# A dense count loop without scatters beside it, in rounds of five, on one core of Trainium2

## Chip, cores and metric

One core of a Trainium2 chip runs the whole program. The metric is the device time of one launch in microseconds (us). The engines are named as in the profile: PE is TensorE (PEld its weight loads), DVE is VectorE, ACT is ScalarE, POOL is GpSimd, SP is the engine that issues most DMA transfers. A q behind a name (DVEq) is that engine's sequencer, which reads instructions, waits on semaphores and loads registers.

## The reference

Four blocks of a graph network with dense layers between them, on x of 3125 nodes by 256 columns and one list of 50,000 edges (src, dst):

```python
x = x + _L0_gnn_ref(_layernorm(x), ..., edge_index)           # two GCN layers over (src, dst)
x = x + _L0_ffn_ref(_layernorm(x)[None], ..., L0_ffn_edge_index)[0]   # a GAT over 32,768 own edges gates 4 experts
x = x + _L1_gnn_ref(_layernorm(x), ..., node_type_4, edge_type_8, src, dst)   # HGT attention
x = x + _L1_ffn_ref(_layernorm(x)[None], ...)[0]              # soft mixture of 8 experts with two hidden layers
x = x + _L2_gnn_ref(_layernorm(x), ..., edge_index)           # SAGE over dst -> src
x = x + _L2_ffn_ref(_layernorm(x)[None], ...)[0]
x = x + _L3_gnn_ref(_layernorm(x), edge_weight, ..., src, dst)  # weighted sum over edges, by src
x = x + _L3_ffn_ref(_layernorm(x)[None], ...)[0]
```

Three orders of edges are needed: the common edges by dst (first GCN and HGT), the 32,768 own edges of the GAT by their dst, and the common edges by src (the weighted sum near the end).

## The kernel before

**Sorting.** An `EdgeSort` computes for every edge the place it has in the sorted list. The list `edge` is then put in order inside the chip. The lists `own` and `back` are put in order by scatters: an indirect DMA issued by POOL writes one column of 128 records (16 bytes each) to their places in DRAM. `own` has 256 such columns and `back` has 391, so 647 scatters in all. The method `send(pool, lo, hi, pace)` issues the columns lo to hi, and behind each one POOL clears a small "pace" buffer of 128x320 numbers, which spaces the scatters in time. The records and addresses that the scatters read must stay in SBUF until they are sent: those of `own` lie in the first of the four large buffers (`bufs[0]`), those of `back` in `back_space`, 128x1955 numbers. The sorted lists come back with `fetch()`: `own` right behind the GCN, `back` late, behind the SAGE block.

**Where the scatters stand.** They are handed out as `beside` functions, which POOL runs in a block of the program while the other engines do that block's work. A block ends for all engines when the last one is through, POOL too. Before the change: `own` 0 to 158 beside the sorts and the first GCN steps; `own` 158 to 256 and `back` 0 to 100 beside the counts; `back` 100 to 160 and 160 to 205 beside the two GCN passes; `back` 205 to 391 beside the experts of the GAT block, and there POOL goes on with `order.write`, the list of nodes by type for HGT.

**The counts.** `build_counts` makes the dense 3200x3200 matrix that says how many edges run from each source to each target. The sorted edges are in groups of 128. A "visit" is one group in one half of the sources for one tile of targets: there are 440 visits. For each visit DVE makes two one-hot matrices from the edges' ends, a narrow one (`hot_d`, L742, 128x128) and a wide one (`hot_s`, L749, 128x1600), and PE multiplies them in four matmuls (L767: 512, 512, 512 and 64 columns), adding into PSUM. When a tile and half (a "bucket", 50 of them, so 8.8 visits each) is done, ACT copies it out (L783), clears the PSUM region (L786) and narrows the copy to 16 bits (L787); SP stores both. There are two PSUM regions, one for each half.

**Rounds.** The loop runs in rounds of RING visits, two rounds to one turn of the loop. At the start of each round DVE's sequencer loads the visits' numbers (bucket and column) into registers from SBUF (the helper's line L96), PE's sequencer loads its own (region), and DVE makes the round's `hot_d`. `hot_s` has RING buffers: a `hot_s` waits until PE is done with the visit RING places earlier, and until ACT has cleared the region that its bucket wants. These waits stand on DVE's sequencer, so everything behind them on DVE waits too, the next round's register loads among them.

Of the kernel before, what the change touches and what calls it, by code (L numbers as in the profile page):

```python
# [6 lines left out]
F32 = mybir.dt.float32  # L7
# [4 lines left out]
I32 = mybir.dt.int32  # L12
# [5 lines left out]
P = 128  # L18
N = 3125
D = 256  # L20
NT = -(-N // P)
# [12 lines left out]
PACE = 320  # L34
# [25 lines left out]
def gather_sems(nc, stage, what, n):  # L60

    return [nc.alloc_semaphore(f"{stage}_{what}{u}") for u in range(n)]
# [111 lines left out]
def alloc_edges(nc, ctx, name, n_edges, like=None, split=False):  # L174


    most = (n_edges + NT * (P - 1)) // P
    groups = -(-most // (R * DEEP)) * R * DEEP
    e = EdgeList()
    e.name, e.groups, e.split = name, groups, split  # L180
    if like is None:
        e.rec = ctx.enter_context(nc.sbuf_tensor(f"{name}_rec", [P, groups, 4], F32))
        e.src = ctx.enter_context(nc.sbuf_tensor(f"{name}_src", [P, groups], I32))
        e.key = ctx.enter_context(nc.sbuf_tensor(f"{name}_key", [P, groups], I32))
    else:
        e.rec, e.src, e.key = (t[:, 0:groups] for t in (like.rec, like.src, like.key))
    e.tile = ctx.enter_context(nc.sbuf_tensor(f"{name}_tile", [P, groups], F32))
    e.blk = ctx.enter_context(nc.sbuf_tensor(f"{name}_blk", [1, groups], I32))
    e.end = ctx.enter_context(nc.sbuf_tensor(f"{name}_ends", [1, NT], I32))
    e.filled = ctx.enter_context(nc.sbuf_tensor(f"{name}_filled", [P, NT], F32))  # L190
    if split:
        e.visits = -(-(most + NT) // 8) * 8
        e.visit_bucket = ctx.enter_context(nc.sbuf_tensor(f"{name}_visit_bucket", [1, e.visits], I32))
        e.visit_group = ctx.enter_context(nc.sbuf_tensor(f"{name}_visit_group", [1, e.visits], I32))
        e.visit_end = ctx.enter_context(nc.sbuf_tensor(f"{name}_visit_end", [1, 2 * NT], I32))
    e.dram = nc.dram_tensor(f"{name}_sorted", (P * groups + GROUPS_MAX, 4), F32).ap()
    return e


class EdgeSort:  # L200
# [15 lines left out]
    def __init__(self, nc, kit, name, e, dst, space, bufs, inside=False):  # L216
        self.nc, self.kit, self.name, self.e, self.bufs = nc, kit, name, e, bufs
        self.rested, = gather_sems(nc, name, "rested", 1)
        self.rests = 0
        self.dst, self.n = dst, dst.shape[0]  # L220
        self.C = C = -(-self.n // P)
        self.inside = inside
        if inside:
            self.to_part, self.to_group, self.low, self.high = (space[:, k * C:(k + 1) * C] for k in range(4))
            self.rec = self.adr = None
        else:
            self.rec = space[:, 0:C * 4].rearrange("p (c w) -> p c w", w=4)
            self.adr = space[:, C * 4:C * 5].bitcast(I32)
            self.sent = gather_sems(nc, name, "sent", self.SENDS)
# [318 lines left out]
    def send(self, pool, lo, hi, pace=None):  # L548
# [13 lines left out]
        if hi == self.C:  # L562
            for u in range(self.SENDS):
                pool.wait_ge(self.sent[u], 16 * -(-(self.C - u) // self.SENDS))

    def put_inside(self, space, beside):

        nc, kit, e, C, groups = self.nc, self.kit, self.e, self.C, self.e.groups
        BATCH, RING = 8, 8
# [110 lines left out]
def build_counts(nc, kit, e, counts, counts16, bufs, beside):  # L680
# [6 lines left out]

    groups, visits = e.groups, e.visits
    COLUMNS = groups + 1
    RING, OUT = 4, 3  # L690
    BASE = RING + 1
    REGION = 2048
    WIDE = NP - FIRST_HALF
# [1224 lines left out]
    return ap2d.rearrange("e (k p) -> p (e k)", p=P)  # L1918


def soft_moe_stage(nc, kit, A, x, bufs, rdeg_dram):


    b2 = bufs[1]
# [3 lines left out]
    with ExitStack() as c:  # L1928
# [3 lines left out]
        gates = sb("gates", [P, NT, E])  # L1932
# [8 lines left out]
        with ExitStack() as cc:  # L1941
# [5 lines left out]
            with nc.Block() as block:  # L1947
# [31 lines left out]
                def _(act):  # L1979
                    for k, n in enumerate("12"):  # L1980
# [5 lines left out]
        of = lambda name: lambda e: A[name][ds(e, 1), :, :]  # L1986
        expert_mlps(nc, "soft", b2, E, [Mid(of("L1_ffn_W1"), 2, fc, ACT.Relu, par["b1"], par["v1"]),
                                        Mid(of("L1_ffn_W2"), fc, fc, ACT.Relu, par["b2"], par["v2"])],
                    of("L1_ffn_Wo"), bo, gates, x, stats=kit.stats)


BIG = 1e30
# [1954 lines left out]
def program(nc, A, out):  # L3947

    with ExitStack() as ctx:
        kit = Kit()  # L3950
# [16 lines left out]
        with ExitStack() as pair:  # L3967
            bufs = [pair.enter_context(nc.sbuf_tensor(n, [P, NT * D], F32)) for n in ("big1", "big2")] + [big3, big4]
            with ExitStack() as c:
# [1 line left out]
                own = alloc_edges(nc, c, "own", own_dst.shape[0])  # L3971
                n_all = -(-A["src"].shape[0] // P) * 5
                back_space = c.enter_context(nc.sbuf_tensor("back_space", [P, n_all], F32))
                pace = {n: c.enter_context(nc.sbuf_tensor(f"{n}_pace", [P, PACE], F32))[:] for n in ("own", "back")}
                paced = lambda lo, hi, which: lambda pool: which.send(pool, lo, hi, pace)
                with ExitStack() as cc:

# [12 lines left out]
                    back_sort.prepare(A["dst"], weight=A["edge_weight"], beside=paced(105, 145, own_sort))  # L3990
                    g = gcn_first(nc, kit, A, cc, x, bufs, paced(145, 152, own_sort), paced(152, 158, own_sort))

                    def rest(pool):
                        own_sort.send(pool, 158, own_sort.C, pace)
                        back_sort.send(pool, 0, 100, pace)
                    build_counts(nc, kit, edges, counts, counts16, bufs, rest)
                    scale_and_heavy_nodes(nc, kit, g)
                    gcn_stage(nc, kit, g, x, bufs, counts, counts16, counts_t, paced(100, 160, back_sort),
                              paced(160, 205, back_sort))
                    own_sort.fetch()  # L4000
                order.find(A["node_type_4"], c)

                def send_and_order(pool):
                    back_sort.send(pool, 205, back_sort.C, pace)
                    order.write(pool)
                gat_moe_stage(nc, kit, A, x, bufs, own, send_and_order)
            hgt_stage(nc, kit, A, x, bufs, edges, order)
            soft_moe_stage(nc, kit, A, x, bufs, rdeg_dram)
        sage_stage(nc, kit, A, x, big3, big4, counts16, rdeg_dram)
        back_sort.fetch()  # L4010
        with ExitStack() as pair:
# [96 lines left out]
```

## Time and profile before

| | us |
|---|---|
| median of 3 runs | 6159.12 (6157.68 to 6162.46) |
| the profiled execution, its own time | 6162.04 |
| its span in the trace | 6160.4 |
| counts, from the first to the last visit | 537 to 939 of the span |
| experts of the GAT block | 1869 to 2229 |
| experts of the soft mixture | 3611 to 4153 |

The profile is of one execution. The page gives the busy time of each engine over the span and in 40 slices of 154 us; the trace can be asked for a stretch (busy time by engine), for groups of instructions by line, for what each engine waited for, and for single instructions in order of time. In a row "[1.43 <-issue]" is idle time of that engine just before, and what ended it; "issue" is a wait for nothing that the profile shows.

### The profile page before, as it was taken

The page shows a single profiled execution, that of the slowest core. Times are in us where ns is not written, and L with a number is a line of the kernel's source. Part 1 is how long each engine was busy: PE and PEld are TensorE (multiplying, and loading weights), DVE is VectorE, ACT ScalarE, POOL GpSimd, SP SyncE. Part 2 cuts the span into 40 slices and gives each one's busy share as a digit, 9 for nine tenths or more (in the row PEclk, how much of TensorE's full clock was granted, in tenths as well). Part 3 has the DMA queues.
Part 4 walks back from the last instruction along what each step waited for, and adds up shares of the span by engine and source line. Part 5 has one row for each costly group of instructions (what it writes and reads, how often), then busy time and mean ns, then how long its engine had stood idle before and what let it go on. Part 6 is the DMA issues. An engine that isn't in the chain of part 4 may idle for free. (4 is left out here: it accounts for less than half of the span.)

```text
span 6160.4 us, 89090 instructions
## 1 busy us (share of the span) xinstructions
PE 4547.2 (74%) x22985; PEld 3258.0 (53%) x23041; DVE 3500.1 (57%) x7298; ACT 1667.5 (27%) x3845; POOL 2410.6 (39%) x2714
## 2 busy tenths in 40 slices
PE   5866777945558979566659889999999395455558
PEld 1213444634446755345536677778888353355546
DVE  8988993556683245699948634441112333655544
ACT  0863553511102225111100233333222121200022
POOL 0747876527707833577600000001111301477700
PEclk8998998955558989788859989999999597677779
DMA  0002346712210038999947210004333321233400
GB/s 31 2 11 75 153 158 205 230 25 34 32 63 22 8 88 332 316 330 322 286 135 237 79 23 10 10 15 143 99 106 103 96 102 53 70 102 104 99 18 21
DMA packets 392065, 669.88 MB, mean 109 GB/s; under 512 B 115851, under 2 KB 280850, under 8 KB 387242
## 3 DMA queue, kind: packets, MB, share of 16 engines
q1 hardware_dynamic: 295938, 420.30, 21.6%
q0 software_dynamic: 95744, 247.14, 13.0%
q8 instruction: 88, 1.44, 0.1%
q14 instruction: 103, 0.84, 0.0%
q10 hardware_dynamic: 192, 0.15, 0.0%
HBM read 438.59 MB, written 228.81 MB: 108 GB/s over the span
## 5 line engine op out<-in xcount | busy, mean ns | idle before, releaser
L3370 POOL CAST sagel_piece<-x 128x1792 fp32r<-128x1792 f16 (+1 forms) x75 | 112.8, 1503 | 1557.1 <-DMA x<-counts 1137.1
L555 POOL DMA_INDIRECT back_sorted<-back_space x391 | 411.4, 1052 | 240.9 <-POOLq L1758 170.8
L1072 POOL DMA_INDIRECT wsum_a_rows<-table,edge_src x416 | 411.8, 990 | 220.0 <-issue 118.5
L1086 PE MATMUL wsum_a_ps<-wsum_a_hot,wsum_a_rows 128*128 128x128 f32 x1664 | 310.7, 363 | 246.3 <-DMA wsum_a_rows<-table,edge_src 139.7
L2172 POOL DMA_INDIRECT big<-hgt_table,edge_key x416 | 393.3, 945 | 176.4 <-issue 131.1
L1086 PEld LDWEIGHTS wsum_a_ps<-wsum_a_hot,wsum_a_rows 128*128 128x128 f32 x1664 | 285.7, 267 | 271.2 <-DVE big L1113 218.0
L3426 PE MATMUL sagel_ps<-sagel_piece,sagel_high 128*128 128x448 f32 x1050 | 397.8, 379 | 0.8 <-issue 0.8
L555 POOL DMA_INDIRECT own_sorted<-big x256 | 273.3, 1068 | 311.2 <-issue 310.2
L767 PE MATMUL cnt_ps<-cnt_hot_s,cnt_hot_d 128*128 128x512 bf16 (+1 forms) x1705 | 305.9, 333 | 107.3 <-DVE cnt_hot_s L749 107.1
L3426 PE MATMUL sagel_ps<-sagel_piece,sagel_low 128*128 128x448 f32 x1050 | 383.9, 366 | 0.0
L2220 PE MATMUL hgt_s_pq<-big 128*128 x1248 | 230.6, 350 | 167.8 <-DVE hgt_s_tmp L2259 134.0
L2172 POOL DMA_INDIRECT big<-gat_table,own_src x288 | 272.3, 946 | 90.5 <-issue 86.2
L749 DVE TENSOR_SCALAR cnt_hot_s<-cnt_iota,cnt_source 128x1600 bf16<-128x1600 int16 x440 | 303.3, 748 | 1.6 <-ACT cnt_ps L786 0.9
L767 PEld LDWEIGHTS cnt_ps<-cnt_hot_s,cnt_hot_d 128*128 128x128 bf16 x1760 | 161.0, 97 | 252.1 <-issue 130.3
L1882 ACT ACTIVATE soft_h<-soft_ps,soft_b,soft_v 128x320 f32<-128x320 f32 x320 | 197.5, 617 | 334.6 <-PE soft_ps L1848 334.6
L2220 PEld LDWEIGHTS hgt_s_pq<-big 128*128 128x128 bf16 x1248 | 145.6, 117 | 236.5 <-issue 187.5
L2249 DVE TENSOR_REDUCE hgt_highest<-hgt_s_pm 128x1024 f32 (+1 forms) x208 | 252.6, 1215 | 0.1
L624 ACT ACTIVATE big<-big 128x128 f16<-128x128 f16 x782 | 228.4, 384 | 22.0 <-DVE big L595 22.0
L2610 PE MATMUL hgt_a_ps<-hgt_a_val,hgt_a_hot 128*128 128x260 f32 x832 | 211.8, 398 | 27.6 <-DVE hgt_a_val L2589 25.6
L1903 DVE TENSOR_TENSOR soft_answer<-soft_py,soft_bo 128x256 f32<-128x256 f32 x200 | 82.8, 414 | 247.1 <-PE soft_py L1860 247.1
L3426 PEld LDWEIGHTS sagel_ps<-sagel_piece,sagel_high 128*128 128x128 f32 x1050 | 197.6, 188 | 18.8 <-issue 1.8
L3426 PEld LDWEIGHTS sagel_ps<-sagel_piece,sagel_low 128*128 128x128 f32 x1050 | 197.7, 188 | 16.6
(977 smaller groups left out, 10773.7 us busy)
## 6 DMA issues: line engine op xcount, KB each, us to landing
hgt_edge_values<-big SPq DMA_DIRECT2D x104, 512.0 KB
big<-hgt_edge_values SPq DMA_DIRECT2D x104, 512.0 KB, 4.5
x<-counts SPq DMA_DIRECT2D x75, 448.0 KB, 3.3
x<-counts SPq DMA_DIRECT2D x75, 336.0 KB, 2.9
counts<-big SPq DMA_DIRECT2D x25, 832.0 KB
counts<-big SPq DMA_DIRECT2D x25, 768.0 KB
big<-counts SPq DMA_DIRECT2D x30, 640.0 KB
counts_turned<-big SPq DMA_DIRECT2D x30, 640.0 KB, 4.0
```

The source lines that it names most:

```text
L555: self.nc.gpsimd.indirect_dma_start(self.e.dram, bass.IndirectOffsetOnAxis(ap=self.adr[:, c:c + 1], axis=0), self.rec[:, c, :], None).then ...
L624: nc.scalar.activation(valued[k % RING][:, n, :], parts[b % 2][:, k % BATCH, :], ACT.Copy, scale=value[:, k:k + 1]).then_inc(weighed, 1)
L749: nc.vector.tensor_scalar(hot_s[u][:], iota16[:], source[:, ds(places[u], 1)], None, ALU.is_equal).then_inc(matched, 1)
L767: mm = nc.tensor.matmul(ps[:, ds(regions[u] + lo, n)], hot_d[h][:, u, :], hot_s[u][:, lo:lo + n], start=False, stop=False, skip_group_chec ...
L1072: nc.gpsimd.indirect_dma_start(rows[n % DEEP][:, u, :], None, table, bass.IndirectOffsetOnAxis(ap=e.src[:, g:g + 1], axis=0)).then_inc(gat ...
L1086: mm = nc.tensor.matmul(ps[r.slot % 2][u][:, k * P:(k + 1) * P], rows[r.slot][:, u, k * P:(k + 1) * P], hot[r.slot % 2][:, u, :], start=Tr ...
L1882: nc.scalar.activation(h[n][:, f, half * CHUNK:(half + 1) * CHUNK], ps[g % RING][:, 0:CHUNK], m.func, bias=bias, scale=scale).then_inc(rea ...
L2172: nc.gpsimd.indirect_dma_start(rows[n % DEEP][:, u, :], None, at.table, bass.IndirectOffsetOnAxis(ap=at.index[:, g:g + 1], axis=0)).then_i ...
L2220: mm = nc.tensor.matmul(pq_v[:, u, :], hot_t[nxt.slot][:, u, :], part[:, ds(blocks[u], 1), :].rearrange("p o w -> p (o w)"), start=(k == 0 ...
L2249: nc.vector.tensor_reduce(highest[:, :, ds(old.n * R + 2 * pair, 2)], pm[pair][:].rearrange("p (g h n) -> p h g n", g=2, h=H), AX_X, ALU.m ...
L2610: nc.tensor.matmul(ps[:, ds(regions[u], W)], hot[k % 2][:, u, :], val[k % 2][:, u, :], start=False, stop=False, skip_group_check=True).the ...
L3426: mm = nc.tensor.matmul(ps[BANKS[half][n]][:, 0:w], part[:, t, f * P:(f + 1) * P], piece, start=(t == 0 and m == 0), stop=(t == NT - 1 and ...
```

## The change

Five edits:

1. No scatter stands beside the counts any more. In their place POOL writes the records of `back` from `back_space` to DRAM (`keep`) and moves those of `own` from the large buffer into `back_space` (`take_up`), which is so one buffer for both lists.
2. The counts have RING = 5: five `hot_s` buffers, rounds of five visits. The number of visits is rounded up to a multiple of 10 in place of 8, and is 440 either way; the loop has 44 turns in place of 55.
3. `own` 158 to 214 and 214 to 256 go beside the two GCN passes (56 and 42 scatters in place of 60 and 45).
4. The GAT block's experts first get the records of `back` again from DRAM, and have `back` 0 to 186 beside them (186 scatters, as before).
5. The soft mixture's experts, which had nothing beside them, read the records into a new buffer `back_space_too` and have `back` 186 to 391 beside them (205 scatters).

```diff
@@ alloc_edges
-        e.visits = -(-(most + NT) // 8) * 8
+        e.visits = -(-(most + NT) // 10) * 10
@@ EdgeSort
+    def keep(self, pool, space):
+        self.kept_by = self.nc.dram_tensor(f"{self.name}_kept", (P, 5 * self.C), F32).ap()
+        self.move(pool, space, self.kept_by)
+
+    def take_up(self, pool, space, kept_by=None):
+        C = self.C
+        self.rec = space[:, 0:C * 4].rearrange("p (c w) -> p c w", w=4)
+        self.adr = space[:, C * 4:C * 5].bitcast(I32)
+        self.move(pool, self.kept_by if kept_by is None else kept_by, space)
+
+    def move(self, pool, from_, to):
+        self.moves += 1
+        pool.dma_start(to, from_).then_inc(self.moved, 16)
+        pool.wait_ge(self.moved, 16 * self.moves)
@@ build_counts
-    RING, OUT = 4, 3
+    RING, OUT = 5, 3
@@ soft_moe_stage
-                    of("L1_ffn_Wo"), bo, gates, x, stats=kit.stats)
+                    of("L1_ffn_Wo"), bo, gates, x, beside=beside, stats=kit.stats)
@@ program
-                pace = {n: c.enter_context(nc.sbuf_tensor(f"{n}_pace", [P, PACE], F32))[:] for n in ("own", "back")}
+                pace_one = c.enter_context(nc.sbuf_tensor("pace", [P, PACE], F32))
+                pace = {n: pace_one[:] for n in ("own", "back")}
-                    def rest(pool):
-                        own_sort.send(pool, 158, own_sort.C, pace)
-                        back_sort.send(pool, 0, 100, pace)
-                    build_counts(nc, kit, edges, counts, counts16, bufs, rest)
+                    def put_away(pool):
+                        back_sort.keep(pool, back_space[:])
+                        own_sort.take_up(pool, back_space[:, 0:n_own], bufs[0][:, 0:n_own])
+                    build_counts(nc, kit, edges, counts, counts16, bufs, put_away)
                     scale_and_heavy_nodes(nc, kit, g)
-                    gcn_stage(nc, kit, g, x, bufs, counts, counts16, counts_t, paced(100, 160, back_sort),
-                              paced(160, 205, back_sort))
+                    gcn_stage(nc, kit, g, x, bufs, counts, counts16, counts_t, paced(158, 214, own_sort),
+                              paced(214, own_sort.C, own_sort))
                     own_sort.fetch()
                 def send_and_order(pool):
-                    back_sort.send(pool, 205, back_sort.C, pace)
+                    back_sort.take_up(pool, back_space[:])
+                    back_sort.send(pool, 0, 186, pace)
                     order.write(pool)
-            soft_moe_stage(nc, kit, A, x, bufs, rdeg_dram)
+            with ExitStack() as c:
+                back_space = c.enter_context(nc.sbuf_tensor("back_space_too", [P, n_all], F32))
+                pace_too = {"back": c.enter_context(nc.sbuf_tensor("back_pace_too", [P, PACE], F32))[:]}
+                def send_rest(pool):
+                    back_sort.take_up(pool, back_space[:])
+                    back_sort.send(pool, 186, back_sort.C, pace_too)
+                soft_moe_stage(nc, kit, A, x, bufs, rdeg_dram, send_rest)
```

The order of DVE's instructions at the start of a round of the counts, before; L96 is the register load, L740 a wait, and each ISA row is the part of the next instruction that puts a register into its address:

```order
L96 TENSOR_LOAD cnt_column0
L740 REGISTER_ALU
L742 ISA
L742 TENSOR_SCALAR cnt_hot_d1<-cnt_iota0,cnt_target0 128x128
L742 ISA
L742 TENSOR_SCALAR cnt_hot_d1<-cnt_iota0,cnt_target0 128x128
L742 ISA
L742 TENSOR_SCALAR cnt_hot_d1<-cnt_iota0,cnt_target0 128x128
L742 ISA
L742 TENSOR_SCALAR cnt_hot_d1<-cnt_iota0,cnt_target0 128x128
```

The same place in the changed kernel, whose lines stand 20 lower:

```order
L96 TENSOR_LOAD cnt_column0
L760 REGISTER_ALU
L762 ISA
L762 TENSOR_SCALAR cnt_hot_d1<-cnt_iota0,cnt_target0 128x128
L762 ISA
L762 TENSOR_SCALAR cnt_hot_d1<-cnt_iota0,cnt_target0 128x128
L762 ISA
L762 TENSOR_SCALAR cnt_hot_d1<-cnt_iota0,cnt_target0 128x128
L762 ISA
L762 TENSOR_SCALAR cnt_hot_d1<-cnt_iota0,cnt_target0 128x128
L762 ISA
L762 TENSOR_SCALAR cnt_hot_d1<-cnt_iota0,cnt_target0 128x128
```

The loads stand there once for five visits, and the first wide one-hot of the round comes behind five narrow ones in place of four.

POOL's instructions around the counts in the changed kernel (the IOTA belongs to the counts' first block, L3300 is the first step behind them; `big` is the large buffer that held `own`):

```order
L734 IOTA big 128x1600
L731 UNCONDITIONAL_BRANCH
L821 UNCONDITIONAL_BRANCH
L583 DMA back_kept<-back_space 128x1955
L583 DMA back_space<-big 128x1280
L735 UNCONDITIONAL_BRANCH
L54 ISA x15
L1612 UNCONDITIONAL_BRANCH
L3300 DMA big<-counts,heavy_at 24x3200
```

Before, 198 pairs of a scatter (L555) and a clear (L560) stood between those branches where the two transfers stand now. And POOL's instructions at the start of the soft mixture's experts, where before it had none; L2192 is the last gather of HGT:

```order
L2192 DMA big<-hgt_table,edge_key 128x512 x416
L2160 UNCONDITIONAL_BRANCH
L54 ISA x72
L1836 UNCONDITIONAL_BRANCH
L583 DMA back_space_too<-back_kept 128x1955
L556 DMA back_sorted<-back_space_too 53688x4
L561 MEMSET back_pace_too 128x320
L556 DMA back_sorted<-back_space_too 53688x4
L561 MEMSET back_pace_too 128x320
```

The transfer stands ahead of the scatters, and they wait for it.

## Rows read from the trace of the kernel before

**Rows 1.** The page: the span.

```profile
span 6160.4 us, 89090 instructions
```

**Rows 2.** Busy time by engine: the counts, their part with scatters, their part without.

```profile
core 0: us, PE busy (x) PEld busy (x) DVE busy (x) ACT busy (x) POOL busy (x), PEclk, DMA share, GB/s
537.00:939.00 402.00, 305.94 (x1705) 161.04 (x1760) 389.34 (x880) 223.88 (x199) 320.79 (x388) 0.99 0.39 152
545.00:890.00 345.00, 262.91 (x1474) 139.72 (x1521) 344.12 (x762) 194.83 (x173) 310.51 (x376) 1.00 0.40 154
894.00:934.00 40.00, 31.99 (x180) 16.15 (x185) 34.12 (x95) 22.30 (x20) 0.00 (x0) 1.00 0.40 163
```

**Rows 3.** DVE's one-hots, 545 to 890 us: busy us, mean ns, idle before.

```profile
L749 DVE TENSOR_SCALAR cnt_hot_s<-cnt_iota,cnt_source 128x1600 bf16<-128x1600 int16 x380 | 267.9, 763 | 0.0
L742 DVE TENSOR_SCALAR cnt_hot_d<-cnt_iota,cnt_target 128x128 bf16<-128x128 int16 x382 | 93.1, 514 | 1.4 <-PE cnt_ps L767 1.0 <-issue 0.3
```

**Rows 4.** Both one-hots, 894 to 934 us.

```profile
L749 DVE TENSOR_SCALAR cnt_hot_s<-cnt_iota,cnt_source 128x1600 bf16<-128x1600 int16 x48 | 27.3, 631 | 0.9 <-ACT cnt_ps L786 0.9
L742 DVE TENSOR_SCALAR cnt_hot_d<-cnt_iota,cnt_target 128x128 bf16<-128x128 int16 x47 | 8.7, 250 | 4.9 <-PE cnt_ps L767 4.9
```

**Rows 5.** PE's weight loads in order of time, beside scatters: one round, x16.

```profile
862.52 2.58 PEld L767 LDWEIGHTS cnt_ps<-cnt_hot_s,cnt_hot_d 128*128 128x128 bf16 x16 [1.07 <-issue]
```

**Rows 6.** The same behind the last scatter: half a round, then five rounds.

```profile
899.98 1.24 PEld L767 LDWEIGHTS cnt_ps<-cnt_hot_s,cnt_hot_d 128*128 128x128 bf16 x8
902.65 2.58 PEld L767 LDWEIGHTS cnt_ps<-cnt_hot_s,cnt_hot_d 128*128 128x128 bf16 x16 [1.43 <-issue]
905.55 2.58 PEld L767 LDWEIGHTS cnt_ps<-cnt_hot_s,cnt_hot_d 128*128 128x128 bf16 x16 [0.32 <-issue]
909.19 2.58 PEld L767 LDWEIGHTS cnt_ps<-cnt_hot_s,cnt_hot_d 128*128 128x128 bf16 x16 [1.06 <-issue]
912.29 2.58 PEld L767 LDWEIGHTS cnt_ps<-cnt_hot_s,cnt_hot_d 128*128 128x128 bf16 x16 [0.52 <-issue]
916.25 2.58 PEld L767 LDWEIGHTS cnt_ps<-cnt_hot_s,cnt_hot_d 128*128 128x128 bf16 x16 [1.38 <-issue]
```

**Rows 7.** Register loads of four numbers and of one, 894 to 934 us: ns min/median/max.

```profile
L96 PEldq TENSOR_LOAD <-cnt_region x12: 329/332/930, 894.6 to 932.2; - x12
...
L96 ACTq TENSOR_LOAD <-edge_visit_end x5: 274/278/382, 898.2 to 925.4; - x5
```

**Rows 8.** GAT experts in order of time: POOL's first scatter, first step behind the scatters, last step.

```profile
1869.27 1.00 POOL L555 DMA_INDIRECT back_sorted<-back_space  x1 [170.84 <-POOLq L1758]
...
2160.52 1.63 POOL L2989 DMA_DIRECT2D type_list<-type_none  x1 [1.76 <-issue]
...
2224.86 0.29 POOL L2997 TENSOR_SCALAR type_source<-type_at 128x28 int32<-128x28 int32 x1 [3.93 <-DMA type_at<-type_list]
```

**Rows 9.** PE there: first matmul, a group beside scatters, one behind them.

```profile
1875.90 11.16 PE L1848 MATMUL gatx_ps<-big,gatx_w 128*128 x32 [28.72 <-DMA gatx_wl<-in_L_ffn_W_dram]
...
1912.78 8.78 PE L1848 MATMUL gatx_ps<-big,gatx_w 128*128 x32
...
2192.04 8.78 PE L1848 MATMUL gatx_ps<-big,gatx_w 128*128 x32
```

**Rows 10.** DVE's last work in that block.

```profile
2228.36 0.43 DVE L1911 BATCH_NORM_STATS2 row_stats<-x  x1
```

**Rows 11.** A transfer from DRAM: KB, us from issue to landing.

```profile
edge_rec<-back_sorted SPq DMA_DIRECT2D x1, 832.0 KB, 4.3
```

**Rows 12.** Soft mixture: PE's first matmul, and its first matmul behind the block.

```profile
3616.22 7.09 PE L1848 MATMUL soft_ps<-big,soft_w 128*128 x16 [12.02 <-DMA soft_wl<-in_L_ffn_Wo_dram]
...
4153.52 0.47 PE L874 MATMUL sage_ln_ps<-ident,sage_ln_st 128*128 128x128 f32 x1 [9.14 <-DVE sage_ln_st L846]
```

**Rows 13.** Second GCN pass: POOL's last clear, DVE's last work.

```profile
1231.41 0.38 POOL L560 MEMSET back_pace<- 128x320 f32 x1
...
1241.41 0.89 DVE L1734 TENSOR_TENSOR big<-gcn_ps,big 128x512 f32<-128x512 f32 x2 [0.59 <-PE gcn_ps L1368]
```

More of the change, by code:

```diff
@@ L218, in __init__ @@
         self.rested, = gather_sems(nc, name, "rested", 1)
-        self.rests = 0
+        self.rests = self.moves = 0
+        self.moved, = gather_sems(nc, name, "moved", 1)
         self.dst, self.n = dst, dst.shape[0]
@@ L1918, in columns, with soft_moe_stage @@
     return ap2d.rearrange("e (k p) -> p (e k)", p=P)
-def soft_moe_stage(nc, kit, A, x, bufs, rdeg_dram):
+def soft_moe_stage(nc, kit, A, x, bufs, rdeg_dram, beside):
     b2 = bufs[1]
```

## The prediction, as recorded before the run

> **What bounds the kernel now.** The page first: the span of 6160.4 us [rows 1] is a row of stages, one behind the other, so what an edit is worth is read in the stage that it touches. The stage at stake is the counts, from 537 to 939 us. I read it by stretches: 402 us for 440 visits, with DVE busy for 389.34 of them and PE for 305.94 [rows 2]. POOL's scatters end some 45 us ahead of the counts (POOL is busy for 310.51 of 345 us, then for 0.00 of 40 [rows 2]), so this trace holds both cases: beside scatters (545 to 890) and without (894 to 934).
>
> Beside scatters DVE is busy for 344.12 of 345 us and makes 380 wide one-hots, 0.908 us for each visit [rows 2, 3]. It is the bound: a round in PE's row of weight loads is 2.58 us of work and 1.07 us of waiting, 3.65 us for four visits [rows 5]. Without scatters the same instructions are shorter. A wide one-hot takes 631 ns in place of 763, a narrow one 250 in place of 514 [rows 3, 4]. Rows overlap a little, so I go by DVE's busy time: 34.12 us for 48 visits [rows 2, 4], which is 0.711 us a visit. If that alone decided, 440 visits would take 313 us. But DVE then stood idle for 5.9 of the 40 us, 4.9 of it behind PE [rows 4]: the bound has moved into the hand-over between the two.
>
> PE's rows without scatters show how. Eight loads (two visits) take 1.24 us and sixteen 2.58, so a visit is 0.67 us of PE [rows 6]. Between rounds PE stands still for a short time in the middle of a turn (0.32 and 0.52 us) and a long one at the loop's branch (1.43, 1.06, 1.38, mean 1.29). Four rounds, 902.65 to 916.25, take 13.60 us: 0.85 us a visit. That is nearer to PE's 0.67 than to anything that DVE needs, and the loss is at the edges of rounds.
>
> **What the change does to the counts.** Two parts.
>
> *No scatters.* This alone would give the pace of the clean stretch: 0.85 times 440 is 374 us, a gain of 28. The 48 visits in 40 us (0.833) would give 367.
>
> *Rounds of five.* The loads and the branch come once in five visits, and DVE may be five visits ahead of PE in place of four. Why the second counts: DVE's last wide one-hot of a round waits until PE is done with the round before, on DVE's sequencer; only then can the sequencer go on to the branch, the two register loads, and the next round's narrow one-hots. With four places PE has four visits (2.7 us) of work left at that moment. What DVE has to do till the next round can start is two loads (0.34 us each at the median of such a load, 0.94 at worst, as PE's and DVE's are alike), the narrow one-hots (8.7 us over 47, 0.18 each, so 0.7), one wide one (0.63) and the branch: 2.4 to 3.4 us, so it is late at some branches. With five places PE has 3.35 us left against 2.6 to 3.6. It should be late rarely, and then PE's own gap decides. In the middle of a turn that is 0.42 (mean of 0.32 and 0.52); at the branch it lies between 0.42 and 1.29, and I take the middle, 0.85, since part of the 1.29 is DVE's lateness. A round of five is 2.58 + 0.67 = 3.25 us of loads, so a turn is 2 x 3.25 + 0.42 + 0.85 = 7.77 us for ten visits, 0.777 a visit, 342 us in all. With the gap of 1.29 kept it is 0.821 and 361 us. Slow register loads still happen (930 ns at worst against 329 at best [rows 7]), so I put the counts at 348 us: 54 less than 402.
>
> A register load takes 333 ns for four numbers (332 in this stretch) and 278 for one [rows 7], so a fifth costs about 18 ns, nothing against a saved load in five. The Trainium skill, Runtime: NRT & Kernel Launch, Instruction fetch mechanics, puts a register load at about 200 ns for each register. By that a round of five would save nothing on the loads, since five numbers cost 1.0 us where four cost 0.8, and DVE would be late at every branch: that is the first rival below. The rows here show under half of that price at four numbers, and nearly none for the fifth.
>
> *The two transfers.* `keep` and `take_up` in the counts are 1.0 MB and 0.66 MB. The nearest row is 832 KB landed in 4.3 us [rows 11]; with queueing I allow 15 us for both. They lie beside 348 us of counts in which POOL has nothing else, so they cost 0; without that cover it would be those 15. ACT, which must clear a region before DVE goes on, was busy for 22.3 of 40 us [rows 2] and held DVE back for 0.9 [rows 4].
>
> **The other stages.**
>
> *GCN.* 56 and 42 scatters for 60 and 45. In the second pass POOL's last clear is at 1231.41 and DVE's last work of the pass at 1241.41 [rows 13]. Fewer scatters end no later, even with the wait for the last landings, so 0.
>
> *GAT experts.* The records (1.0 MB) must come back ahead of the first scatter. Scaled from 832 KB in 4.3 us it would be 5.2, and it is issued beside 2 MB of expert weights, so I take 9 us. POOL starts its scatters that much later than 1869.27. It is nearly the last in this block: its last step is at 2224.86 to 2225.15, DVE's at 2228.36 to 2228.79 [rows 8, 10]. It gets 1.8 us back, the wait for landed scatters ahead of `type_list` [rows 8], which now comes elsewhere. So POOL ends at 2225.15 + 9 - 1.8 = 2232.4, 3.5 us behind DVE's old end. DVE's own end moves too: PE waits for its first weights until 1875.90 [rows 9], and a third of the traffic more delays it by 2 to 3 us. The two delays lie side by side, so the larger counts: +3.5 us (0 if the transfer takes 5 us, +8 if 13). HGT, which waits for this block, starts that much later.
>
> *Soft mixture.* 205 scatters more. In the GAT's experts 186 took 289.5 us (from 1869.27 to 2160.52 less its wait of 1.76 [rows 8]), 1.56 each, so 319 us and the transfer; the block lasts from 3616.22 to about 4153 [rows 12], 537 us. POOL is through 200 us early. What do scatters do to the others there? In the GAT block a group of 32 matmuls takes 8.78 us beside scatters and 8.78 behind them [rows 9]. PE binds, and is not slowed. So only the transfer beside the first weights costs, +2.5 us (0 to 4).
>
> **The sum.** -54 + 0 + 3.5 + 2.5 = -48 us. Against the profiled execution: span 6160.4 to 6112.4, own time 6162.04 (1.6 outside the span) to 6114. That execution stands 2.9 above the median of 6159.12, so the forecast for the median is 6111 us.
>
> **The rivals.**
>
> *The fifth place brings nothing (17 in 100).* The counts take the clean stretch's pace, 367 to 374 us, a little less for 22 branches in 110 saved. For it: DVE's loads at a branch take up to 0.94 us each, and PE's gap there may be all its own. Against it: the mid-turn gaps are 0.3 to 0.5, with the same loads and no branch. Gain 28 to 35, less 6: 6130 to 6137 us.
>
> *DVE's pace alone (8 in 100).* All gaps vanish behind the fifth buffer and the counts take 313 us. For it: DVE's 0.711 is the longer of the two bare times. Against: PE's sequencer can't start a round's matmuls ahead of its own load. 6159 - 89 + 6 = 6076 us.
>
> *ACT becomes the bound (4 in 100): no change.* DVE, five visits ahead, runs into the wait for the cleared region at each of the 50 buckets. At the 0.9 us of [rows 4] each, 45 us of the 54 are lost: 6156. Against: a bucket has 8.8 visits, about 6.9 us, while ACT's busy 22.30 us for 48 visits [rows 2] are 4.1 us a bucket.
>
> *Slower (4 in 100): the soft experts suffer.* If scatters held DVE or ACT there as they hold DVE in the counts, PE would wait for free PSUM banks in each of 40 groups of five tiles. It decides from 1.2 us a group (48 / 40) and at 2 us a group the time is 6111 + 80 = 6191. For it: wide one-hots are 21% longer beside scatters [rows 3, 4]. Against: 8.78 and 8.78 [rows 9].
>
> **How the numbers follow.** The forecast case has 67 in 100 and gives 6095 to 6126 (counts 332 to 361, the two transfers 1 to 9). What a measurement of this kernel can tell from no change is about 0.2%, 12 us. The first rival reaches to 6140, and with part of the second the range is 6086 to 6140; out of it lie most of the second, the third and the fourth. Faster by over 0.2%: 67 + 17 + 8, less a little, 91 in 100. Within 0.2%: 5. Slower: 4.
>
> **What would show it.** Counts from first to last visit near 348 us; wide one-hots at 631 ns throughout; PE's gaps 0.3 to 0.5 in mid-turn and below 1 at the branch; POOL's last step behind DVE's in the GAT block; the groups of matmuls in the soft experts as long with scatters as they were without. The prediction is wrong if branch gaps stay at 1.3, if DVE waits for ACT in most buckets, or if a stage that the change doesn't touch runs at another clock.

## The result and the profile after

The changed kernel takes 6243.21 us (median of 4 runs, 6237.74 to 6249.4) where the kernel before takes 6158.40 beside it: a ratio of 1.0137, 95% interval 1.0122 to 1.0152. It is 85 us slower; 6111 was forecast.

The page's span answers to [rows 1]:

```profile
span 6247.7 us, 88910 instructions
```

The busy time by stretch answers to [rows 2]; the last row is the whole of the counts, from the first narrow one-hot to the last weight load.

```profile
core 0: us, PE busy (x) PEld busy (x) DVE busy (x) ACT busy (x) POOL busy (x), PEclk, DMA share, GB/s
545.00:890.00 345.00, 245.16 (x1265) 115.73 (x1296) 236.43 (x648) 165.08 (x147) 0.00 (x0) 0.93 0.32 129
894.00:934.00 40.00, 27.18 (x136) 12.57 (x140) 27.21 (x77) 18.05 (x16) 0.00 (x0) 0.91 0.30 123
542.00:1016.00 474.00, 335.59 (x1714) 158.16 (x1759) 322.06 (x880) 220.86 (x196) 0.00 (x0) 0.92 0.31 127
```

POOL is idle, as planned, yet everybody else is idle more too: DVE for 109 of the 345 us in which it was busy throughout in [rows 2]. By the same measure (first narrow one-hot to last weight load) the counts took 398.4 us before and take 474.2 now, 76 more. The rest of the span's 87 us is small: 5 us lie ahead of the counts and come and go between executions (the counts begin at 536 or 541 us in runs with the same program up to there), 3 in the GAT experts, 3 in the soft mixture, some single ones elsewhere.

DVE's one-hots in the counts, by form, answer to [rows 3, 4]:

```profile
L769 DVE TENSOR_SCALAR cnt_hot_s<-cnt_iota,cnt_source 128x1600 bf16<-128x1600 int16 x436 | 246.1, 630 | 2.1 <-ACT cnt_ps L806 1.5 <-PE cnt_ps L787 0.3 <-issue 0.2
L762 DVE TENSOR_SCALAR cnt_hot_d<-cnt_iota,cnt_target 128x128 bf16<-128x128 int16 x435 | 78.6, 249 | 148.8 <-PE cnt_ps L787 104.2 <-issue 44.5
```

The work itself is what the forecast said: 630 and 249 ns. The 148.8 us of idleness ahead of the narrow one-hots is new, and PE waits for DVE in its turn. A chain that goes round between two engines, each idle, has something in it that is on neither engine's busy row. It is on the sequencers'. The register loads (ns min/median/max) answer to [rows 7]:

```profile
L96 DVEq TENSOR_LOAD <-edge_visit_bucket x87: 587/1187/2523, 543.9 to 1008.6; - x87
...
L96 DVEq TENSOR_LOAD <-cnt_column x87: 586/1189/2590, 545.2 to 1009.9; - x87
L96 PEldq TENSOR_LOAD <-cnt_region x87: 584/1236/2647, 546.4 to 1010.9; - x87
L96 ACTq TENSOR_LOAD <-edge_visit_end x49: 273/278/402, 552.9 to 999.7; - x49
```

A load of five numbers takes 584 ns at least and 1187 to 1236 at the median, where four took 333 to 346. It is not dear everywhere: sorted by where it begins, 17 of the 22 column loads that begin at a multiple of 16 bytes (every fourth round, since five numbers are 20 bytes) take under 1 us, and none of the other 66 takes less than 1181 ns. And the trace of before held it already, in a stage that the prediction never looked at: DVE's five loads of five numbers each in the GAT layer. In order of time they take 612, 1196, 1178, 1181 and 591 ns: the first and the last, which begin at byte 0 and byte 80 of their row, are the short ones.

```profile
L96 DVEq TENSOR_LOAD <-gat_t_last x5: 591/1178/1196, 1716.0 to 1722.6; - x5
```

PE's weight loads in order of time answer to [rows 6]:

```profile
675.80 3.25 PEld L787 LDWEIGHTS cnt_ps<-cnt_hot_s,cnt_hot_d 128*128 128x128 bf16 x20 [1.54 <-issue]
681.67 3.25 PEld L787 LDWEIGHTS cnt_ps<-cnt_hot_s,cnt_hot_d 128*128 128x128 bf16 x20 [2.62 <-issue]
687.86 0.49 PEld L787 LDWEIGHTS cnt_ps<-cnt_hot_s,cnt_hot_d 128*128 128x128 bf16 x3 [2.94 <-issue]
688.63 0.15 PEld L787 LDWEIGHTS cnt_ps<-cnt_hot_s,cnt_hot_d 128*128 128x128 bf16 x1 [0.28 <-issue]
689.05 0.21 PEld L787 LDWEIGHTS cnt_ps<-cnt_hot_s,cnt_hot_d 128*128 128x128 bf16 x2 [0.27 <-issue]
```

A round of five is 3.25 us of loads, to the hundredth what was forecast; the gaps are 1.5 to 2.9 us and not 0.4 to 0.9. Behind two such gaps the loads are suddenly 0.43 us apart. The granted clock beside them says why: 0.50 of full speed, 1.2 GHz, for these three microseconds, and 1.00 ahead of them and behind.

```profile
681.00:687.00 6.00, 3.33 (x19) 1.69 (x20) 3.49 (x10) 2.81 (x2) 0.00 (x0) 1.00 0.49 197
688.00:691.00 3.00, 3.00 (x10) 1.25 (x10) 2.64 (x9) 0.00 (x0) 0.00 (x0) 0.50 0.00 0
```

In the whole loop 151 loads follow the one before in their round by 0.3 to 0.45 us (8 in the kernel before), 102 of them within a visit and 49 from one visit to the next; together they are 30 us longer than at the usual distance. The lower clock follows PE's idleness here, and adds to the time.

### The profile page after: what moved, and what is told of

It reads as the page before. It is cut to its first block and busy times, and to the rows that moved or that the text cites. A ratio compares the mean times of both kernels' runs of the same rounds, so it can differ in the third digit from the quotient of the medians.

```text
span 6247.7 us, 88910 instructions
## 1 busy us (share of the span) xinstructions
PE 4597.9 (74%) x22996; PEld 3272.4 (52%) x23041; DVE 3442.6 (55%) x7298; ACT 1669.2 (27%) x3845; POOL 2370.5 (38%) x2718
## 5 line engine op out<-in xcount | busy, mean ns | idle before, releaser
L1106 PE MATMUL wsum_a_ps<-wsum_a_hot,wsum_a_rows 128*128 128x128 f32 x1664 | 328.1, 377 | 231.4 <-DMA wsum_a_rows<-table,edge_src 137.9
L2192 POOL DMA_INDIRECT big<-hgt_table,edge_key x416 | 393.8, 947 | 177.3 <-issue 131.7
L787 PE MATMUL cnt_ps<-cnt_hot_s,cnt_hot_d 128*128 128x512 bf16 (+1 forms) x1716 | 336.0, 356 | 153.0 <-DVE cnt_hot_s L769 152.4
L1106 PEld LDWEIGHTS wsum_a_ps<-wsum_a_hot,wsum_a_rows 128*128 128x128 f32 x1664 | 302.6, 281 | 256.9 <-DVE big L1133 184.7
L2192 POOL DMA_INDIRECT big<-gat_table,own_src x288 | 272.7, 947 | 90.5 <-issue 86.2
L556 POOL DMA_INDIRECT own_sorted<-big x158 | 164.9, 1044 | 293.7 <-issue 293.7
L769 DVE TENSOR_SCALAR cnt_hot_s<-cnt_iota,cnt_source 128x1600 bf16<-128x1600 int16 x440 | 248.3, 630 | 2.1 <-ACT cnt_ps L806 1.5
L556 POOL DMA_INDIRECT back_sorted<-back_space_too x205 | 208.6, 1018 | 40.9 <-issue 33.8
```

What stands on the lines that cost most here:

```text
L556: self.nc.gpsimd.indirect_dma_start(self.e.dram, bass.IndirectOffsetOnAxis(ap=self.adr[:, c:c + 1], axis=0), self.rec[:, c, :], None).then ...
L769: nc.vector.tensor_scalar(hot_s[u][:], iota16[:], source[:, ds(places[u], 1)], None, ALU.is_equal).then_inc(matched, 1)
L787: mm = nc.tensor.matmul(ps[:, ds(regions[u] + lo, n)], hot_d[h][:, u, :], hot_s[u][:, lo:lo + n], start=False, stop=False, skip_group_chec ...
L1106: mm = nc.tensor.matmul(ps[r.slot % 2][u][:, k * P:(k + 1) * P], rows[r.slot][:, u, k * P:(k + 1) * P], hot[r.slot % 2][:, u, :], start=Tr ...
L2192: nc.gpsimd.indirect_dma_start(rows[n % DEEP][:, u, :], None, at.table, bass.IndirectOffsetOnAxis(ap=at.index[:, g:g + 1], axis=0)).then_i ...
```

## The experiments

Theory A: the slower load of five numbers is the whole loss, because most rounds no longer begin at a multiple of 16 bytes (A1), or because of the fifth number itself (A2). Rivals: the counts without scatters have a slow pace of their own (B), or the fifth place is worth nothing (D). All runs in one table; the counts from the first narrow one-hot to the last weight load, the load being DVE's of `column` (or its copy) at the median, the clock from 545 to 890 us. Load, clock and counts are of one traced execution of each kernel; the ratio is of whole times.

| kernel | places, numbers a load, rounds a turn | scatters beside | load, ns | clock | counts, us | ratio to before, 95% |
|---|---|---|---|---|---|---|
| before | 4, 4, 2 | yes | 343 | 1.00 | 398.4 | 1 |
| changed | 5, 5, 2 | no | 1189 | 0.93 | 474.2 | 1.0137 (1.0122 to 1.0152) |
| e1_four | 4, 4, 2 | no | 343 | 1.00 | 372.0 | 0.9957 (0.9940 to 0.9973) |
| e2_five_beside | 5, 5, 2 | yes | 1187 | 0.94 | 480.5 | 1.0123 (1.0106 to 1.0140) |
| e3_rows_of_eight | 5, 5 aligned, 2 | no | 590 | 1.00 | 385.4 | 1.0008 (0.9994 to 1.0023) |
| e4_four_shifted | 4, 4 shifted, 2 | no | 966 | 0.91 | 529.0 | 1.0211 (1.0194 to 1.0228) |
| e5_fours_five_places | 5, 4, 10 | no | 342 | 1.00 | 345.5 | 0.9929 (0.9916 to 0.9942) |
| e7_fours_five_beside | 5, 4, 10 | yes | 345 | 1.00 | 394.5 | 1.0005 (0.9996 to 1.0013) |
| e8_fours_early_load | 5, 4, 10, PE's early | no | 343 | 1.00 | 348.5 | 0.9932 (0.9920 to 0.9945) |
| e10_fours_eight_places | 8, 4, 10 | no | 342 | 0.99 | 344.2 | 0.9931 (0.9914 to 0.9947) |
| e11_fours_ten_rounds | 4, 4, 10 | no | 342 | 1.00 | 354.9 | 0.9947 (0.9931 to 0.9964) |

The kernel before took 6520 us beside e1 to e4, 6593 beside e5, e7 and e8, and 6163 beside e10 and e11. At the first two of these levels stages with gathers from DRAM are longer (from HGT's first step to the first weight load of the soft mixture: 1387 us in the trace of before, 1555 in e2's, 1611 in e5's, 1390 in e11's), but not the counts. The cause isn't known: the chip is not enough for it, since e5 and e11 have the same chip on record. So the counts are compared in us, and whole times by their ratios.

### Undoing the five, undoing the removal: e1_four and e2_five_beside

```diff
-    RING, OUT = 5, 3
+    RING, OUT = 4, 3
```

> The changed kernel with rounds of four and four places for wide one-hots; everything else as changed. Theory A (a load of five numbers is what costs: 587 ns at least, 1182 to 1237 in most rounds, where four took 333 to 343): the loads are back at 333 to 343 ns and the counts take the pace of the stretch without scatters, 0.83 to 0.85 us a visit, 367 to 374 us; the time is the changed kernel's 6243 less some 105, 6135 to 6145. Rival B (something else of the change slows the counts: the lone pace without scatters, or the clock): the counts stay above 402 us and the time above 6165.

372.0 us, as A said, and B is out: without scatters the loop is faster, not slower. By the ratio the kernel is 28 us faster than before, where the counts lost 26. e2 is the kernel before with this edit (and the fifth place in a free part of a big buffer):

```diff
-    RING, OUT = 4, 3
+    RING, OUT = 5, 3
```

> The kernel before with rounds of five and five places (the fifth in a free part of a big buffer), scatters beside the counts as before. Theory A: loads of five take 0.59 us in one round of four and about 1.2 in the others, and with wide one-hots of 0.76 us the counts are no shorter than the changed kernel's 478 us: 480 to 520, the time 6235 to 6275. Rival B (five is harmless, the missing scatters did it): counts at 385 to 402 us, the time 6140 to 6158.

480.5 us, the lower end of A's 480 to 520. The loads of five cost 82 us beside scatters and 76 net of the removal's gain without: with them in the loop it hardly matters whether POOL is there.

### Address or number: e3_rows_of_eight and e4_four_shifted

```diff
+                for to, of in ((region8, region), (column8, column), (bucket8, e.visit_bucket)):
+                    link(nc.vector.tensor_copy(to[:].rearrange("o (k n) -> o k n", n=8)[:, :, 0:RING],
+                                               of[:].rearrange("o (k n) -> o k n", n=RING)))
...
-                        regions = numbers(nc, mybir.EngineType.PE, region[0:1, ds(first, RING)], REGION)
+                        regions = numbers(nc, mybir.EngineType.PE, region8[0:1, ds((j * 2 + h) * 8, RING)], REGION)
```

> The changed kernel, where the numbers of each round of five stand in a row of eight, so that every load of five begins at a multiple of 32 bytes (three copies of 440 numbers more ahead of the loop, under 3 us). Theory A1 (where the load begins is what costs): all loads take about 590 ns, a quarter us more than four numbers; the counts come to 350 to 370 us, the time to 6115 to 6140. Rival A2 (any load of five is slow in most rounds, whatever its address): loads of 1.2 us stay, counts about 478, the time 6240 to 6250.

The copies stand in a free part of a big buffer, so the profile calls them by its name. All loads of five are short now, in the trace of e3 from 545 to 880 us:

```profile
L96 DVEq TENSOR_LOAD <-big x156: 583/590/1776, 546.6 to 879.4; - x156
L96 PEldq TENSOR_LOAD <-big x77: 579/584/1716, 547.7 to 877.8; - x77
```

The counts fall by 88.8 us from the change of address alone, the granted clock is back at 1.00, and A1 stands. At 385.4 us they stayed above the 350 to 370 expected, because even an aligned fifth number costs a quarter of a microsecond. e4 does the opposite, with rounds of four:

```diff
+                for to, of in ((region1, region), (column1, column), (bucket1, e.visit_bucket)):
+                    link(nc.vector.tensor_copy(to[:, 1:visits + 1], of[:]))
...
-                        regions = numbers(nc, mybir.EngineType.PE, region[0:1, ds(first, RING)], REGION)
+                        regions = numbers(nc, mybir.EngineType.PE, region1[0:1, ds(first + 1, RING)], REGION)
```

> The kernel of rounds of four without scatters, where the numbers of all visits stand one place (4 bytes) later, so that no load of four begins at a multiple of 16 bytes. Theory A1: loads of four take some 965 ns (as four of the seven loads of type_weights do in both kernels), 0.6 more than aligned; with two loads on DVE's path a round and one on PE's, 110 rounds cost 70 to 130 us more than with aligned loads, counts 440 to 500, the time 6205 to 6270. Rival A2 (five is what costs, not the address): loads of 333 to 343 ns, counts 367 to 374, the time as with aligned loads of four.

```profile
L96 DVEq TENSOR_LOAD <-big x140: 958/966/2274, 546.2 to 879.6; - x140
L96 PEldq TENSOR_LOAD <-big x69: 997/1003/2267, 547.6 to 876.2; - x69
```

Four bytes of offset make four numbers cost 966 ns and not 343, and the counts 529.0 us in place of 372.0. That is more than the 440 to 500 expected. Two terms more than cover the 157 us: 110 rounds by two loads on DVE, one behind the other, by 0.62 us are 137, and the lower clock (191 late weight loads, worked out as above) makes 38. In PE's row the gaps between rounds are 114 us longer in sum than e1's, and the rounds themselves 43. So most of DVE's pair of loads is on the path, and the rest is hidden. The loads of `type_weights` that the expectation leans on are no example of the address: all seven begin at multiples of 16 bytes, and in the trace of before the first takes 329 ns and the other six 946 to 970. They belong to the long loads named at the end.

### The load by itself: e6_loads_alone and e9_loads_used

> Nothing but register loads: 1 to 8 numbers, four times each, beginning 0, 4, 8 and 12 bytes behind a multiple of 16, on DVE and TensorE; the output is zeros and all the reference's work is left out. Theory A1: aligned, 1 to 4 numbers take 280 to 345 ns and 5 some 590; off by 4 to 12 bytes 4 numbers take about 960 and 5 about 1180 to 1230. If the time goes by single numbers where it is not aligned, 2 take about 500 and 3 about 730. Rival A2 (only the number counts): the same times at all four offsets.

Nothing used the numbers, and the trace holds no load at all: the run says nothing. e9 uses each number once.

```diff
+                        for again in range(4):
+                            for k, v in enumerate(numbers(nc, mybir.EngineType.DVE, row[0:1, 16 + at:16 + at + n], 1)):
+                                c = ((at * 8 + n - 1) * 4 + again) * 8 + k
+                                nc.vector.tensor_copy(taken[0:1, c:c + 1], used[0:1, ds(v, 1)])
```

> Register loads by themselves: 1 to 8 numbers, four times each, beginning 0, 4, 8 and 12 bytes behind a multiple of 16, on DVE and TensorE, each number used by a small instruction; the output is zeros and all the reference's work is left out. Theory A1: aligned, 1 to 4 numbers take 280 to 345 ns and 5 some 590; off by 4 to 12 bytes 4 numbers take about 960 to 1000 and 5 about 1180 to 1230. Rival A2 (only the number counts): the same times at all four offsets.

Its loads in order of time, ns min/median/max: aligned with 4, 5 and 8 numbers, then 4 bytes further with 4, 5 and 8.

```profile
L96 DVEq TENSOR_LOAD <-row x4: 341/343/361, 36.6 to 39.1; - x4
L96 PEldq TENSOR_LOAD <-row x4: 332/336/340, 36.6 to 39.3; - x4
...
L96 DVEq TENSOR_LOAD <-row x4: 585/590/605, 41.1 to 44.7; - x4
...
L96 DVEq TENSOR_LOAD <-row x3: 594/605/608, 63.9 to 67.0; - x3
...
L96 DVEq TENSOR_LOAD <-row x4: 960/960/961, 85.0 to 89.4; - x4
L96 PEldq TENSOR_LOAD <-row x4: 994/996/999, 85.1 to 89.7; - x4
...
L96 DVEq TENSOR_LOAD <-row x4: 1178/1180/1186, 92.2 to 97.5; - x4
...
L96 DVEq TENSOR_LOAD <-row x4: 1842/1844/1849, 123.6 to 132.0; - x4
```

All medians on DVE, for 1 to 8 numbers: aligned 315, 524, 744, 343, 590, 812, 1027, 602; 4 bytes further 299, 517, 743, 960, 1180, 1398, 1623, 1844, and the same to 7 ns at 8 and at 12 bytes. Read it as: one number is 300 ns, each further one 220 (232 on PE), except that four in a row from a multiple of 16 bytes count as one (with up to 80 ns on top when more follow: 590 for five, 524 for two). A2, by which the address would not matter, is out. And one thing nobody expected: two or three aligned numbers (524 and 744) cost more than four (343). Eight that begin 4 bytes off hold an aligned four inside, and get nothing for it.

### What the fifth place is worth: e5, e11, e7, e10, e8

e5 separates the places from the loads: `ROUND = 4` numbers a load, five places gone through in turn, ten rounds written out a turn.

```diff
-                with dve.Fori(0, visits // RING // 2) as j:
-                    for h in range(2):
-                        first = (j * 2 + h) * RING
+                with dve.Fori(0, visits // ROUND // 10) as j:
+                    for h in range(10):
+                        first = (j * 10 + h) * ROUND
...
-                            nc.vector.tensor_scalar(hot_s[u][:], iota16[:],
+                            nc.vector.tensor_scalar(hot_s[(h * ROUND + u) % RING][:], iota16[:],
```

> The changed kernel with its five places for wide one-hots, but rounds and loads of four numbers each, aligned to 16 bytes; ten rounds are written out for each turn of the loop, and the wide one-hots go round the five places. Theory A (the fifth place is worth what the prediction said, the loads of five took it away): loads of 333 to 343 ns, gaps of 0.3 to 0.5 us between rounds, counts 330 to 350 us, 0.990 to 0.993 of the kernel before. Rival D (the fifth place brings nothing, the first rival of the prediction): counts at the 372 us of four places without scatters, 0.995 to 0.997.

345.5 us, and 0.9929 of the time before: among the fastest with e8 and e10, and some 2% under the changed kernel (0.9929 / 1.0137 = 0.979). PE's weight loads in e5:

```profile
702.72 2.58 PEld L787 LDWEIGHTS cnt_ps<-cnt_hot_s,cnt_hot_d 128*128 128x128 bf16 x16 [0.40 <-issue]
705.59 2.58 PEld L787 LDWEIGHTS cnt_ps<-cnt_hot_s,cnt_hot_d 128*128 128x128 bf16 x16 [0.29 <-issue]
708.45 2.58 PEld L787 LDWEIGHTS cnt_ps<-cnt_hot_s,cnt_hot_d 128*128 128x128 bf16 x16 [0.29 <-issue]
711.92 2.58 PEld L787 LDWEIGHTS cnt_ps<-cnt_hot_s,cnt_hot_d 128*128 128x128 bf16 x16 [0.89 <-issue]
```

Gaps of 0.3 to 0.4 us, and 0.89 where PE's own load took 0.89. e11 is e5 with four places:

```diff
-    RING, OUT, ROUND = 5, 3, 4
+    RING, OUT, ROUND = 4, 3, 4
```

> As the run with five places and loads of four without scatters, ten rounds written out for each turn, but with four places: what the fifth place brings apart from the branches saved. Theory A (the fifth place is what brings it): counts 365 to 372 us as with four places and two rounds a turn, 0.995 to 0.997 of the kernel before. Rival F (the branches saved bring it, 11 in place of 55): counts 345 to 350, 0.992 to 0.994.

354.9 us is neither. From 372.0 to 354.9 it is the turns saved (55 to 11, 0.39 us each), from 354.9 to 345.5 the fifth place: 17 us and 9. Both A's "the fifth place brings it" and F are half right. The split rests on one trace each: the ratios of e1, e11 and e5 (0.9957, 0.9947, 0.9929) stand in the same order, but the interval of e11 overlaps with both others.

e7 puts the same loop beside the scatters:

> The kernel before, scatters beside the counts, with that same loop: five places, rounds and loads of four, ten rounds a turn. Theory A (beside scatters DVE's wide one-hots bind, 0.908 us a visit): counts 385 to 398 us, 0.997 to 1.000 of the kernel before. Rival E (the hand-over binds there too): counts 340 to 370, 0.990 to 0.995.

394.5 us for 398.4, and no difference in the time. Beside scatters DVE is busy for 344.53 of the 345 us (545 to 890), and hand-over and branches are worth 4 us of counts: the fifth place pays only once the scatters are gone. e10 has eight places, and five buffers for narrow one-hots in place of two:

```diff
-    RING, OUT, ROUND = 5, 3, 4
+    RING, OUT, ROUND, ENDS = 8, 3, 4, 5
```

> As the run with five places and loads of four, with eight places for wide one-hots and five buffers for narrow ones (the added ones in free parts of big buffers). If some lateness of the one engine for the other is left with five places (34 to 38 of 250 us in waits of DVE and TensorE for each other), the counts come nearer to DVE's own 0.711 us a visit: 320 to 335 us, 0.988 to 0.992. Rival G (each engine stands behind its own register loads now, which no place hides): 340 to 348 us, 0.992 to 0.994.

e8 is e5 with PE's load two visits early:

```diff
+                            if u == 2 and h < 9:
+                                coming = load(first + ROUND)
```

> As the run with five places and loads of four without scatters, but TensorE's load for the next round is issued two visits early (not across a turn's branch). If TensorE's own load is what it stands still for between rounds (0.33 us and up, 99 of 110 rounds), the counts lose another 25 to 35 us: 305 to 320. If it waits for DVE there, or DVE's 0.711 us a visit binds (313 us), the counts stay within 8 us of the run without the early load.

344.2 and 348.5 us for 345.5: both within a few us, and rival G and the second case hold. The waits from 600 to 850 us, first e5's and then e8's, show what e8 did (us, times, longest):

```profile
PE cnt_ps L787 <- DVE cnt_hot_s L769: 19.6, 32, 1.3
DVE cnt_hot_d L762 <- PE cnt_ps L787: 10.1, 13, 1.3
DVE cnt_hot_d L762 <- issue: 7.3, 21, 0.7
```

```profile
DVE cnt_hot_d L762 <- PE cnt_ps L791: 17.7, 32, 1.0
PE cnt_ps L791 <- DVE cnt_hot_s L769: 9.8, 20, 1.1
PE cnt_ps L791 <- issue: 8.9, 22, 0.7
```

PE waits less for DVE and stands inside the round in place of between rounds, DVE waits more for PE. DVE is busy for 231 of 250 us in both, so little is left to win here.

## Why the prediction was wrong

**The step that failed** is the price of the fifth number: "A register load takes 333 ns for four numbers and 278 for one, so a fifth costs about 18 ns". Two points, one at each end of a function with a step between, were joined by a line. Four numbers were cheap because every load of the counts before began at a multiple of 16 bytes. The fifth costs 250 ns there, and 850 elsewhere; rounds of five begin elsewhere three times in four. By these values a mean load is (590 + 3 x 1180) / 4 = 1030 ns and not 350 (measured on DVE, with the long ones: 1321, and 458 before). What was built on it falls with it: that DVE is ready again within 2.6 to 3.6 us, while PE has 3.35 us of work left. Two loads of 1.18 in place of 0.34 make the 2.6 some 4.3 us, later than PE's end of work. PE's gaps are 2.1 us in the middle of a turn and 1.4 at the branch (medians), where 0.3 to 0.5 and below 1 were named; the second round of a turn never begins at a multiple of 16 bytes.

In sum, two loads on DVE in 88 rounds are 120 us more, and the lower clock's 30 come on top. Part of these 150 is hidden: against e3, with the same rounds and short loads, PE's gaps are 56 us longer in sum and the rounds themselves 33. Against e5, which has the same five places with loads of four and 33 branches fewer, the changed kernel's counts are 129 us longer: 89 for the address (e3) and 40 for the aligned fifth number and the branches together.

The direction was to be had from what was at hand. The Trainium skill, Runtime: NRT & Kernel Launch, Instruction fetch mechanics, puts the runtime's register loads, which come from HBM, at about 200 ns for each register. The prediction weighed that against one row, saw 333 ns for four, and dropped it; it also gave the rule only a no-gain rival, by pricing four and five both at its rate. The runs of this case, whose loads come from SBUF, show about that rate (220 and 232 ns a number) for every number outside an aligned four, and not for an aligned four (343 ns in all). The rival that was missing worked with the rows: it takes the measured price for four and 200 ns a number for five, 1.0 us. By it each load grows by 0.67 us, and 88 rounds by two loads on DVE are 118: 6111 + 118 = 6229 us, slower by 70.

**The rest of the counts held.** Wide one-hots 630 ns (631 forecast); 372.0 us for the removal alone (367 to 374); a round of five 3.25 us; and with cheap loads e5 comes to 345.5 us, where the forecast's 348, counted to the same end (398.4 in place of 402), is 344. But the reason was only half right, so that the number came out so near is in part luck: the forecast gave all of it to the fifth place and a saved branch in five, and e11 shows 17 us of 27 in the branches. PE's gaps were said to be lateness of DVE at branches; in e5 they are largely PE's own load, and where that is slow (0.89 us), the gap is.

**The transfers.** `keep` and `take_up` cost nothing in the counts: POOL issues them at 530.4 and 534.8 us, ahead of the first one-hot, and idles behind them. In the GAT experts POOL's record transfer and first scatter, PE's first matmul, POOL's last step and DVE's last work, which answer to [rows 8 to 10]:

```profile
1946.53 0.59 POOL L583 DMA_DIRECT2D back_space<-back_kept  x1 [170.34 <-POOLq L1778]
1953.56 1.03 POOL L556 DMA_INDIRECT back_sorted<-back_space  x1 [6.44 <-DMA back_space<-back_kept]
...
1955.24 11.79 PE L1868 MATMUL gatx_ps<-big,gatx_w 128*128 x32 [30.53 <-DMA gatx_wl<-in_L_ffn_W_dram]
...
2303.46 0.29 POOL L3017 TENSOR_SCALAR type_source<-type_at 128x28 int32<-128x28 int32 x1 [3.74 <-DMA type_at<-type_list]
...
2308.35 0.43 DVE L1931 BATCH_NORM_STATS2 row_stats<-x  x1
```

The transfer takes 7.0 us (9 assumed), POOL's last step begins 4.9 us ahead of DVE's, where the forecast had POOL end 3.5 us behind DVE's old end, and the block is 2.6 us longer (3.5 forecast), by the later weights. The soft mixture is 3.2 us longer (2.5), and its groups of matmuls, 4.47 us beside scatters, are as they were. e1 has these transfers and e2 has not, on one chip: their medians differ by 103 us and their ratios by 0.0166 (108 us), their counts by 108.5, which leaves 0 to 6 us for the transfers.

## What to carry to other kernels

Read registers in aligned groups of four, and keep the loop's size and the ring's size apart: places can be five while loads stay four. Before a count in a load, a transfer or a tile is changed, look for that very count anywhere in the trace, also in stages that the change doesn't touch, and don't draw a line through two sizes. When two engines wait for each other and neither is busy, read their sequencers' rows.

## What the runs showed that was not expected

- A register load of 1 to 8 numbers follows a rule with a step: about 300 ns and 220 more for each further number, unless four stand from a multiple of 16 bytes, which count as about one. Aligned, four (343) are cheaper than two (524).
- Within the kernel some loads are 260 or 600 ns longer than that at any size (e5: 339 at least, 346 at the median, 964 at most; in e9, with nothing beside, four aligned numbers took 361 at most). The last six of the seven loads of `type_weights`, which stand 25 to 29 us apart, are all of that kind (946 to 970). What makes them long stays open.
- Idle gaps of 1.5 to 3 us between TensorE's rounds came with a granted clock of 0.50 for some microseconds, which made the matmuls 30 us longer in all; with gaps of 0.3 to 1.5 (e1, e5) it stayed at 1.00.
- A turn of the loop less was worth 0.39 us (e1 to e11, with 110 rounds of loads in both), on engines that were over 85% busy. The branch itself takes 0.06 us on DVE and 0.21 on PE there; what makes up the rest isn't shown.
